# Routed experts in full and half lots: the first layer's expert stage rewritten

## The reference

```python
xf = x.reshape(-1, Cc)                                   # 8192 x 128
logits = jax.nn.relu(xf @ Wr1 + br1) @ Wr2 + br2
gates = jax.nn.softmax(logits, axis=-1)
tg, ti = jax.lax.top_k(gates, K)                         # K = 2 of E = 8
tg = jax.nn.softmax(tg / K, axis=-1)
out = jax.nn.silu(xf @ Ws1 + bs1) @ Ws2 + bs2            # the shared expert
for e in range(E):
    h = jax.nn.silu(xf @ We1[e] + be1[e]) @ We2[e] + be2[e]   # 128 -> 512 -> 128
    w = jnp.sum(tg * (ti == e), axis=-1)
    out = out + w[:, None] * h
```

## Time and profile before

| | |
|---|---|
| median of 3 runs | 1253.32 us (1247.99 to 1254.52) |
| profiled execution | 1253.19 us, its span 1251.3 us |
| granted TensorE clock, mean | 0.957 of 2.4 GHz |
| PE busy in the span | 1126.2 us (90%) |
| PEld | 812.2 us (65%) |
| DVE | 890.3 us (71%) |
| ACT | 649.0 us (52%) |
| POOL | 735.5 us (59%) |
| `grouped`, first transposition to last weight load | 468.7 to 751.4 us |

### The profile page before, as it was taken

How to read it: one execution, slowest core, us unless ns; L and a number is a source line. 1 busy time by engine, 2 the same in 40 slices (tenths; PEclk the granted TensorE clock), 3 DMA queues, 4 the chain that set the end, 5 groups by cost and what they waited for, 6 DMA issues and landing times. The chain is left out here.

```text
span 1251.3 us, 26693 instructions
## 1 busy us (share of the span) xinstructions
PE 1126.2 (90%) x9302; PEld 812.2 (65%) x9302; DVE 890.3 (71%) x2638; ACT 649.0 (52%) x1057; POOL 735.5 (59%) x908
## 2 busy tenths in 40 slices
PE   3954999999999969999999998999879899899994
PEld 2642555555555438899999896777646667667773
DVE  8996888888888636666666564888784489874442
ACT  4941777777777744444444344555533265553331
POOL 3204788777887743555555452344438567638886
PEclk9975999999999989999999998999889999999998
DMA  9904000000000012222222223222348312265543
GB/s 325 365 1 183 24 28 28 28 28 24 28 26 28 26 40 57 68 68 70 69 73 69 61 60 101 68 68 65 105 139 251 107 44 71 78 214 84 71 54 30
DMA packets 96813, 104.07 MB, mean 83 GB/s; under 512 B 12812, under 2 KB 84300, under 8 KB 96588
## 3 DMA queue, kind: packets, MB, share of 16 engines
q1 hardware_dynamic: 75792, 75.10, 19.5%
q0 software_dynamic: 19968, 26.63, 8.9%
q10 hardware_dynamic: 956, 1.04, 0.3%
HBM read 55.58 MB, written 47.15 MB: 82 GB/s over the span
## 5 line engine op out<-in xcount | busy, mean ns | idle before, releaser
L838 ACT ACTIVATE probs<-ps 128x1024 f32<-128x1024 f32 x256 | 254.5, 1025 | 112.7 <-PE ps L747 109.6
L1040 POOL DMA_INDIRECT slots<-rowbuf,slots x192 | 206.8, 1077 | 62.3 <-issue 36.0
L1151 POOL DMA_INDIRECT y<-slot_y,where x144 | 150.8, 1047 | 146.2 <-DVE slot_y L1132 122.7
L1219 ACT ACTIVATE slot_h<-ps,own 128x256 f32<-128x256 f32 x288 | 120.5, 470 | 154.5 <-PE ps L1183 152.8
L1183 PE MATMUL ps<-slot_x,own 128*128 128x256 f32 x576 | 141.6, 390 | 4.2 <-DVE slot_x L1121 3.9
L1195 PEld LDWEIGHTS ps<-own,slot_h 128*128 128x128 f32 x1152 | 140.5, 193 | 3.8
L764 PE MATMUL ps<-probs,vext 128*32 128x256 f32 x2048 | 139.5, 391 | 3.1 <-issue 3.1
L1195 PE MATMUL ps<-own,slot_h 128*128 128x128 f32 x1152 | 140.6, 276 | 0.0
L1530 PE MATMUL ps<-xT,packs 128*128 128x512 f32 x256 | 120.8, 610 | 11.6 <-ACT h L1702 11.6
L1702 ACT ACTIVATE h<-ps,packs 128x512 f32<-128x512 f32 x128 | 85.5, 685 | 86.9 <-PE ps L1530 84.3
L1183 PEld LDWEIGHTS ps<-slot_x,own 128*128 128x128 f32 x576 | 105.5, 193 | 20.6 <-DVE slot_x L1121 8.9
(11 more groups left out here) (302 smaller groups left out, 2211.4 us busy)
## 6 DMA issues: line engine op xcount, KB each, us to landing
toeplitz<-conv_kernel SPq DMA_DIRECT2D x16, 1024.0 KB, 7.1
slots<-blank SPq DMA_DIRECT2D x26, 528.0 KB, 8.8
slot_rows<-slots SPq DMA_DIRECT2D x72, 132.0 KB, 2.1
routed<-y SPq DMA_DIRECT2D x32, 256.0 KB, 3.1
packs<-in_experts SPq DMA_DIRECT2D x1, 4624.0 KB, 14.2
packs<-in_experts SPq DMA_DIRECT2D x8, 578.0 KB, 8.0
xT<-slots SPq DMA_DIRECT2D x16, 264.0 KB, 2.8
stream<-in_x SPq DMA_DIRECT2D x8, 512.0 KB, 8.5
```

The source lines that it names most:

```text
L838: act.activation(probs[:, p % 4, :, :, :].rearrange("p j k t -> p j (k t)"), ps[:, 2 * (p % 2):2 * (p % 2) + 2, :], ACT.Exp, scale=DK ** - ...
L1040: return pool.indirect_dma_start(m["slot_dram"][layer], bass.IndirectOffsetOnAxis(ap=where, axis=0), m["rowbuf"][:, tile, :], None)
L1151: pool.indirect_dma_start(m["y_dram"][layer], bass.IndirectOffsetOnAxis(ap=where[:, j, h:h + 1], axis=0), y[:, j, h, :], None).then_inc(se ...
L1219: ins = act.activation(hidden[:, j % 2, k, :], ps[:, 2 * (j % 2) + k // 2, (k % 2) * LOT:(k % 2) * LOT + LOT], act_func, bias=own[:, j, P_ ...
```

## The change

The 72 lots of 256 rows become 60 full lots of 256 rows and 15 half lots of 128 rows. An expert's rows are rounded up to 128 now: as many full lots as fit, and one half lot for an odd rest. The worst case is 64 full lots and 7 half ones over; the full ones past the 60th are done as two half lots each. Every fifth step is a half lot (`is_half`), `lot_of` gives the step's place in the table. `staggered` writes all 75 steps out, with no hardware loop on any engine; SP's loads are written out too. VectorE's `get_own` is cut in two: the register load and the copy of the weights stay at the front, the four small operations become `weigh`, which comes last in the step, behind take_x and put_y. SP's load of rows waits until turn of lot t-4 is done (`turned`) instead of out. `place_two` has more operations for the new slot numbers and table.

```diff
+WHOLE = 2 * TOKENS // LOT - E // 2
+HALF_LOTS = 2 * (2 * TOKENS // LOT - WHOLE) + E - 1
+STEPS = WHOLE + HALF_LOTS
...
-def staggered(engine, steps, count=GROUPS, buffers=2):
...
-    with engine.Fori(0, (count - peeled) // buffers) as r:
...
+def staggered(steps):
...
+    for i in range(STEPS + max(lag for _, lag in steps)):
         for step, lag in steps:
...
+            if 0 <= i - lag < STEPS:
+                step(i - lag, (i - lag) % UNROLL)
+
+
+def is_half(t):
+
+    return t % 5 == 4
+
+
+def lot_of(t):
+
+    return WHOLE + t // 5 if is_half(t) else t - t // 5
```

In `place_two` (VectorE; `link` waits for the operation before the next, `did` does not):

```diff
-                c.link(ts(tmp, size, 1.0 / LOT, 0.5 - 0.5 / LOT, ALU.mult, ALU.add))
...
-                c.link(stt(place[:, :, :], start.unsqueeze(1).broadcast_to([P, TILES, E]),
-                           float(LOT), place[:, :, :], ALU.mult, ALU.add))
+                c.link(ts(tmp, size, 1.0 / P, 0.5 - 0.5 / P, ALU.mult, ALU.add))
...
+                c.link(ts(pairs, tmp, 0.5, -0.25, ALU.mult, ALU.add))
+                c.link(ts(pairs, pairs, MAGIC, None, ALU.add))
+                c.link(ts(pairs, pairs, -MAGIC, None, ALU.add))
+                c.did(dve.tensor_tensor_scan(end, ones[:, 0:E], pairs, 0.0, ALU.mult, ALU.add))
+                c.link(stt(odd, pairs, -2.0, tmp, ALU.mult, ALU.add))
+                c.did(tt(start, end, pairs, ALU.subtract))
+                c.did(ts(far, end, end[:, E - 1:E], -float(LOT), ALU.subtract, ALU.mult))
+                c.link(dve.tensor_tensor_scan(odd_end, ones[:, 0:E], odd, 0.0, ALU.mult, ALU.add))
+                c.did(ts(start, start, float(LOT), None, ALU.mult))
+                c.did(ts(pairs, pairs, float(LOT), None, ALU.mult))
+                c.link(tt(odd, odd_end, odd, ALU.subtract))
+                c.did(stt(far, odd, float(P), far, ALU.mult, ALU.add))
+                c.link(tt(z[:, :, :], place[:, :, :], wide_e(pairs), ALU.is_ge))
+                c.did(tt(place[:, :, :], place[:, :, :], wide_e(start), ALU.add))
+                c.link(tt(z[:, :, :], z[:, :, :], wide_e(far), ALU.mult))
+                c.link(tt(place[:, :, :], place[:, :, :], z[:, :, :], ALU.add))
...
+                c.did(stt(odd_end, end[:, E - 1:E].broadcast_to([P, E]), 2.0, odd_end, ALU.mult, ALU.add))
...
+                c.link(tt(passed[:, :, :],
+                          cst[:, C_HALF:C_HALF + HALF_LOTS].unsqueeze(2).broadcast_to([P, HALF_LOTS, E]),
+                          odd_end.unsqueeze(1).broadcast_to([P, HALF_LOTS, E]), ALU.is_ge))
+                c.did(dve.tensor_reduce(v[4][:, 0:HALF_LOTS], passed[:, :, :], AX.X, ALU.add))
+                c.link(ts(v[1][:, 0:HALF_LOTS], late, float(E), -float(E), ALU.is_ge, ALU.mult))
+                c.link(tt(late, late, v[4][:, 0:HALF_LOTS], ALU.add))
+                c.link(tt(late, late, v[1][:, 0:HALF_LOTS], ALU.add))
```

In `grouped`:

```diff
-                    sp.wait_ge(sem["downed"], i * UNROLL + j + 1)
-                    sp.wait_ge(sem["weight_ready"], i * UNROLL + j + 1)
...
+                sp.wait_ge(sem["turned"], t + 1)
+                sp.wait_ge(sem["weight_ready"], t + 1)
+                if is_half(t):
+                    sp.dma_start(rows[:, j, 0, :], half_slots[:, lot - WHOLE, :]).then_inc(sem[f"rows{j}"], 16)
+                else:
+                    sp.dma_start(rows[:, j, :, :].rearrange("p h d -> p (h d)"), slots[:, lot, :])\
...
                 dve.tensor_copy(own[:, j, :], packs[:, bass.ds(e, 1), :].rearrange("p e n -> p (e n)"))\
                     .then_inc(sem["own_ready"], 1)
-                dve.wait_ge(sem[f"rows{j}"], rows_loaded(t, j))
+
+            def weigh(t, j):
+                n = halves(t)
+                dve.wait_ge(sem[f"rows{j}"], rows_loaded(t))
 
                 dve.wait_ge(sem["y_free"], t + 1)
...
-            staggered(dve, [(get_own, 0), (take_x, 0), (put_y, 2)], lots, UNROLL)
+            staggered([(get_own, 0), (take_x, 0), (put_y, 2), (weigh, 0)])
...
-                for h in range(HALVES):
+                for h in range(halves(t)):
...
                 for k in range(KI):
-                    ins = pe.matmul(ps[:, 2 * (j % 2) + k // 2, (k % 2) * LOT:(k % 2) * LOT + LOT],
-                                    own[:, j, P * k:P * k + P], xs[:, j % 2, :], start=True, stop=True)
+                    ins = pe.matmul(ps[:, 2 * (j % 2) + k // 2, (k % 2) * n:(k % 2) * n + n],
+                                    own[:, j, P * k:P * k + P], xs[:, j % 2, 0:n], start=True, stop=True)
```

More of the change, by code:

```diff
@@ L54 @@
 SPARE = 4
-BLANK_CHUNKS = [(i, k) for i in range(2) for k in range(LOTS[i] * LOT // (BLANK * P))]
+SLOT_ROWS = (-(-(WHOLE * LOT + HALF_LOTS * P) // (BLANK * P)) * BLANK * P, TOKENS)
+BLANK_CHUNKS = [(i, k) for i in range(2) for k in range(SLOT_ROWS[i] // (BLANK * P))]
 P_DOWN = INTER
@@ L72 @@
 C_COUNT = C_MASK + 128
[L73 to L75 removed]
+C_HALF = C_COUNT + STEPS
+C_TOKEN = C_HALF + HALF_LOTS
+C_END = C_TOKEN + 64
 R_BQK, R_BV, R_BOUT, R_GAMMA, R_BETA = 0, 256, 512, 768, 896
@@ L160, in build @@
         slots = sb("slots", [P, 2, TILES], mybir.dt.int32)
[L161 to L166, removed]
+        table = sb("table", [P, STEPS])
+        table_int = sb("table_int", [P, STEPS], mybir.dt.int32)
+        slot_dram = [nc.dram_tensor(f"slots{i}", [(SLOT_ROWS[i] + i * TOKENS), ROW], F32).ap() for i in range(2)]
+        y_dram = [nc.dram_tensor(f"y{i}", [3 * TOKENS + SLOT_ROWS[i], D], F32).ap() for i in range(2)]
         kernel_dram = nc.dram_tensor("conv_kernel", [P, KPAD], F32).ap()
@@ L242, in first @@
         chosen = sb("chosen", [P, TILES, E], F16)
-        lots = sb("lots", [P, 4, E])
+        lots = sb("lots", [P, 8, E])
         n = TILES * E
@@ L502, in place_two @@
                 places(c, dve, ps, ones, before, place, lots[:, 0, :], COUNTS)
-                size, end, start, tmp = (lots[:, k, :] for k in range(4))
-                c.link(ts(tmp, size, 1.0 / LOT, 0.5 - 0.5 / LOT, ALU.mult, ALU.add))
[L506 to L509, removed]
-                c.link(stt(place[:, :, :], start.unsqueeze(1).broadcast_to([P, TILES, E]),
-                           float(LOT), place[:, :, :], ALU.mult, ALU.add))
+                size, pairs, odd, end, odd_end, start, far, tmp = (lots[:, k, :] for k in range(8))
+                wide_e = lambda t: t.unsqueeze(1).broadcast_to([P, TILES, E])
+                c.link(ts(tmp, size, 1.0 / P, 0.5 - 0.5 / P, ALU.mult, ALU.add))
+                c.link(ts(tmp, tmp, MAGIC, None, ALU.add))
+                c.link(ts(tmp, tmp, -MAGIC, None, ALU.add))
+                c.link(ts(pairs, tmp, 0.5, -0.25, ALU.mult, ALU.add))
[14 more added lines that the diff above has]
+                c.link(tt(place[:, :, :], place[:, :, :], z[:, :, :], ALU.add))
                 for choice, mask in enumerate((mask1, mask2)):
@@ L1047, in grouped @@
     ps, ident = m["ps"], m["ident"]
-    lots = LOTS[layer]
     act_func = (ACT.Silu, ACT.Gelu_apprx_tanh)[layer]
     HALVES = LOT // P
+    halves = lambda t: 1 if is_half(t) else HALVES
+    passed = lambda t: 16 * sum(halves(i) for i in range(t % UNROLL, t, UNROLL))
     with ExitStack() as ctx:
@@ L1167, in _ @@
             pe.sem_inc(sem["upped"], 4)
+            pe.sem_inc(sem["turned"], UNROLL)
             def turn(t, j):
-                pe.wait_ge(sem[f"rows{j}"], rows_loaded(t, j))
+                pe.wait_ge(sem[f"rows{j}"], rows_loaded(t))
                 pe.wait_ge(sem["x_ready"], t + 1)
-                for h in range(HALVES):
+                for h in range(halves(t)):
                     ins = pe.transpose(ps[:, 4 + j % 2, P * h:P * h + P], rows[:, j, h, 0:D], ident)
@@ L1197, in make_out @@
                 ins.then_inc(sem["downed"], 1)
-            staggered(pe, [(turn, 0), (make_hidden, 1), (make_out, 2)], lots, UNROLL)
+            staggered([(turn, 0), (make_hidden, 1), (make_out, 2)])
             pe.wait_ge(m["pack0_loaded"], 16)
```

81 lines of the change are left out of this document (37 added, 44 removed).

## The result

The changed kernel takes 1237.88 us (median of 4 runs, 1237.11 to 1240.37) against 1252.28 for the kernel before, measured with it: a ratio of 0.9892, with a 95% interval of 0.9861 to 0.9924.

A forecast was written before the change was run, and what follows sets the result against it. TensorE was taken to bound the routed stage, VectorE close behind. Stage 252.2 + 12.5 + 4.5 = 269.2 against 282.8, -13.6; first stage +2.6; total -11.0 on 1253.3, so 1242.3 us, range 1234 to 1253.

The forecast's parts named there:

- 14.2 us beside TensorE's work, explained by 12.8 of waits for x: Routed stage before: 282.8 us less 268.6 of TensorE's work leaves 14.2, explained by 24 waits for x.
- The 4.5 that were kept: Routed stage: of the 14.2 us, 4.5 stay, about 3 for the first lots and 1.5 for stray waits.
- TensorE bounds the stage, with 3.73 a full lot: Routed stage: TensorE works without a gap, a full lot's step taking 3.73 us, with VectorE close behind.
- POOL's wait goes with the order: VectorE awaits POOL's signal after put_y, not ahead of x, so the 12.8 us of waits for x mostly go.
- Own 0.76 after the last small operation: VectorE's expert copy starts 0.76 us after the last small weight operation, the register load standing between.
- the widest unknown: The register load's 0.76 in VectorE's chain, bounded by about 0.6 and 1.0, worth -4.5 to +6.7 us.
- Two waits behind each half lot, 0.57 and 0.32: TensorE waits for x twice after each half lot, 0.89 us together, 14 times, 12.5 in all.
- Stage −13.6: Routed stage: 252.2 of work, 12.5 of half-lot waits and 4.5 kept make 269.2 against 282.8 us.
- First stage +2.6: Placement ahead of attention: VectorE's work grows 4.65 us, the landing of stores hides some 2; 2.6 taken.
- Row loads worth nothing: SP's loads waiting for turn, not out, gain nothing: a load lands in 2.2 us, under a 3.73 step.
- Unrolled code at nothing: Some 16 new code blocks for TensorE cost 0 to 1.5 us, taken as 0 within the stray 1.5.
- The rival with a falling clock: Half-lot waits pull TensorE's clock to half, 1.7 us each, 25.5 in all, so 1267.8; chance 6%.

The follow-up runs named there:

- the run with the number ahead: Changed kernel with VectorE's register load of the next expert's number moved right behind the copy of x, one step ahead: 1228.94 us, ratio 0.979.
- the first of the kernels above: Changed kernel with VectorE's four small operations put ahead of x again: 1255.14 us, ratio 1.0011.

## Why the prediction was right, point by point

- *14.2 us beside TensorE's work, explained by 12.8 of waits for x.* Read too simply. The 12.8 in 24 pieces of the earlier trace rows count the matmuls' waits (3.9, 4 times) on top of those of the weight loads (8.9, 20 times), which are in part the same waits. Another part of the 14.2 is the start of the stage, 5.8 us at a granted clock of 0.50. The 4.5 that were kept stand as an allowance and don't follow from the 12.8.
- *TensorE bounds the stage, with 3.73 a full lot.* Right: from the turn at 563.23 to the next at 567.48 there are 4.25, which is 3.73 and the wait of 0.53.
- *POOL's wait goes with the order.* Right, shown by doing and undoing it: 24.1 to 0.7 us, and back to 25.4 with the old order. The stray rest was taken as 4.5; from 270.0, less 252.2 and 14 times 1.05, 3.1 are left (2.4 if the 15.4 of all fourteen pairs are taken). Some 2 of it is again the start: the granted clock is 0.50 until 473.7, 4.2 us of the stage.
- *Own 0.76 after the last small operation.* Measured 0.74 (558.72 to 559.46), so the widest unknown was read rightly from the peeled lots. The load itself is as before in the median, 307 ns. The floor of about 600 ns that the Trainium skill, "DMA: Bandwidth & Descriptors", section "Latency and other measured facts", gives for it isn't seen in its record here either:

```profile
L1125 DVEq TENSOR_LOAD <-table_int x75: 300/307/555, 468.5 to 734.2; - x75
```

- *Two waits behind each half lot, 0.57 and 0.32.* Two waits there are, and the place and the cause are shown by the run with the number ahead, which takes both away. The first is 0.52. The second is the term that was mis-sized: 0.53 instead of 0.32. The step held VectorE to 2.48 from x to the next own; it took 2.69 (560.14 to 562.83). Up to 561.32 the chain goes as planned; then the first small operation, beside a second multiply that is longer than usual (the pair takes 0.71 instead of 0.48), ends late and costs 0.12, and from the last small operation to own it is 0.87 instead of 0.76, another 0.11; the register load in it takes 435 ns instead of 307. It is much the same behind 12 of the 14 half lots. Behind one (the hidden at 599.48) multiply and load have their usual lengths, and the second wait is 0.32, as forecast; behind the remaining one VectorE waited 0.7 for POOL. The chain of the step was right, and what it lacked is these two longer operations. Per half lot 1.05 instead of 0.89, 14 times 0.16, 2.2 us.
- *Stage −13.6.* Measured 282.7 to 270.0, −12.7, by the span of weight loads; −13.9 with the time between the stage's barriers. The two mis-sizings, 2.2 more at half lots and 1.4 less in stray waits, nearly cancel; that the sum came so close is in part luck.
- *First stage +2.6.* Measured +2.53; over all ten profiles attention begins at 100.4 to 100.8 with the new placement and at 98.2 to 99.4 with the old. VectorE's part was counted as 4.65 and is 4.45; what the landing of SP's stores hides was taken as 2 and is 1.92. The stores themselves came 1.23 later, which no step had foreseen, but still ended ahead of VectorE (97.11 against 99.76).
- *Row loads worth nothing.* Wrong in the mechanism, small in the time. The step held a load's 2.2 us against a full step of 3.73 and looked only at TensorE's waits for x. Around half lots the steps are shorter, and with the loads behind out again TensorE waits 11.2 us for rows instead of 4.3; what that is worth, some 2 us at most, isn't sure.
- *Unrolled code at nothing.* Nearly right: the written-out loop alone is 1.0019 of the time before, 2.4 us more, and the whole interval lies above 1 (1.0007 to 1.0031). The instruction queue fetched 75 blocks there and 74 in the changed kernel, instead of 61. VectorE's waits for POOL are longer in that profile too (29.7 for 24.1), so what of the 2.4 us is the code's own cost isn't shown.
- *The clock.* The rival with a falling clock is out. In three windows over the stage of the changed kernel, in the columns told above:

```profile
473.70:556.00 82.30, 79.89 (x554) 73.87 (x554) 53.64 (x195) 37.16 (x97) 42.95 (x39) 1.00 0.23 64
556.00:650.00 94.00, 91.44 (x646) 84.77 (x645) 64.10 (x233) 40.02 (x105) 53.58 (x49) 1.00 0.25 70
650.00:735.00 85.00, 82.04 (x567) 75.87 (x566) 57.23 (x209) 37.02 (x96) 46.75 (x43) 1.00 0.22 64
```

  The half-clock stretch of the kernel before went with the order, as forecast. The three kernels with the old order each have one such fall in mid-stage, to 0.50 for some 3.4 us, and each at the longest wait of the weight loads for x in its stage: 2.1 us before, 3.5 in the first of the kernels above, 2.3 with the loop written out alone. In the seven with the new order the clock stays at 1.00 from its first rise to the end of the stage. The Trainium skill, "TensorE: Matmul & The Clock Gate", section "HAM oscillation — how this bites in real kernels", tells of bursts of matmuls that each begin at the lower clock after a wait for data; the waits of its example are longer than those of the changed kernel. For waits of 0.5 us, the longest 1.1, these windows show nothing of it; on the one of 1.88 in the earlier trace rows (2.1 for the weight loads) a fall did follow.
- *The rest.* The median came out 14.4 lower, the span of the profiled runs 15.5. The stages that the change touches explain 11.4 (−13.9 and +2.5), where 11.0 were forecast. In these two profiles attention is 1.65 shorter and what follows the routed experts 2.5. The change edits nothing there, and both lie inside what these stages vary by between profiles (attention at its lower end). That they are chance is likely, but not shown: what follows the routed experts takes 486.5 to 487.4 in four of the five kernels with half lots and 488.5 to 489.8 in four of the five without, and no run tells why.

## What to carry to other kernels

Work taken off the engine that bounds a stage pays only as far as the next engine can follow: 16.4 us were removed here and 1.5 came out, until a register load and the register operations on it, 0.62 us, left VectorE's chain and 15.7 came out. Before making steps shorter, add up the second engine's chain start to start, loads of registers and their idle time among it, and hold it against the shortest step. And put what others wait for ahead of what may itself have to wait: that order alone, in the old loop and with full lots, gave 6.6 of the stage's 12.7 us. Writing the loop out then gave 4.6 (with the earlier row loads), and the half lots 1.5.

## What the runs showed of the hardware that was not expected

VectorE's operations between two on-chip buffers are not of constant length. The multiply (L1167) takes 286 ns in the median and up to 508:

```profile
L1167 DVE TENSOR_SCALAR slot_y<-slot_y,weight x135: 278/286/508, 478.5 to 740.3; 128x128 f32<-128x128 f32 x135
```

Twelve of the 135 take more than 330 ns, and all twelve start 0.48 us (one 0.64) after a POOL indirect write began and end 0.02 to 0.03 us behind it. So it is in the pair at 560.92: the second multiply starts at 561.13 and takes 0.51, and the write, begun at 560.65, takes until 561.61. Overlap alone doesn't do it. Sixty other multiplies overlap a write at some point and take 291 ns or less, and with the number loaded ahead 89 of 135 overlap one and none takes over 309. The register loads behind the twelve are longer as well, 379 to 446 ns. This is seen, not tested: no run here took the writes away, and the cause stays open.

A turn of the hardware loop costs VectorE 0.52 us between one step and the next (idle time of 1.19 instead of 0.67 ahead of the expert copy). Written out, the copy has 0.57 to 0.59 of idle time in the usual step, and no branch stands ahead of it.
